# The bias of the base product as one more TensorE pass per half

## The reference, cut to what matters

```python
x = x + autocorrelation(layernorm(x), ctx, ctx)            # part a
x = x + ffn0(layernorm(x), W_base, b_base, W_router, A, B)  # part b
x = x + window_attention(layernorm(x), ctx, Wq, ..., bo)    # parts b and c
x = x + ffn1(layernorm(x), A, B, Wr)                        # part c
...
# inside ffn0, for the 128 rows of an item
lora_out = einsum('ner,eor->no', h * combine, B_stack) * SCALING
base_out = xf @ W_base.T + b_base
out = base_out + lora_out
```

## Time and profile before

| what | value |
|---|---|
| three timed executions | 2021.28, 2022.52, 2024.9 us (median 2022.52) |
| the profiled execution | 2025.97 us, of it 2024.1 us in the span |
| TensorE busy | 1855.6 us, 92% of the span |
| VectorE busy | 1519.6 us, 75% |
| ScalarE busy | 1347.2 us, 67% |
| GpSimd busy | 1088.4 us, 54% |
| mean granted TensorE clock | 0.969 |

### The profile page before, as it was taken

How to read it: one execution, slowest core, us unless ns; L and a number is a source line. 1 busy time by engine, 2 the same in 40 slices (tenths; PEclk the granted TensorE clock), 3 DMA queues, 4 the chain that set the end, 5 groups by cost and what they waited for, 6 DMA issues and landing times. The chain is left out here.

```text
span 2024.1 us, 49212 instructions
## 1 busy us (share of the span) xinstructions
PE 1855.6 (92%) x18912; PEld 1131.0 (56%) x18912; DVE 1519.6 (75%) x4529; ACT 1347.2 (67%) x1958; POOL 1088.4 (54%) x902
## 2 busy tenths in 40 slices
PE   4889999999999999999999999999999999999975
PEld 2355555665555655555565655566555565655543
DVE  6677777778777778777877777777777877877743
ACT  4267776677776677776667777667777666777652
POOL 2565555466555466555556655546655645655541
PEclk8899999999999999999999999999999999999985
DMA  5001110011111011111001111001111110111000
GB/s 217 22 33 53 52 52 31 31 52 41 52 52 36 27 50 41 52 52 52 31 31 43 50 52 52 31 31 49 45 52 52 44 39 31 41 52 42 21 6 17
DMA packets 25165, 91.56 MB, mean 45 GB/s; under 512 B 3184, under 2 KB 3312, under 8 KB 24624
## 3 DMA queue, kind: packets, MB, share of 16 engines
q1 hardware_dynamic: 25136, 91.17, 12.8%
HBM read 74.39 MB, written 16.78 MB: 45 GB/s over the span
## 5 line engine op out<-in xcount | busy, mean ns | idle before, releaser
L548 PE MATMUL pb<-w_base_h,even_words 128*128 128x512 f16 x1024 | 324.8, 379 | 0.4 <-ACT mid_t L851 0.4
L1370 POOL TENSOR_TENSOR p_hl<-sc,p_hl 128x512 f16<-128x512 f32 x128 | 178.1, 1391 | 180.3 <-ACT p_hl L730 180.3
L450 PE MATMUL pa<-ctx_a,tab 128*128 128x512 f32 x384 | 203.4, 655 | 35.6 <-ACT q_spec L730 24.3
L840 ACT ACTIVATE q_diag<-sc,par 32x1024 f32<-32x1024 f32 x192 | 216.1, 1141 | 19.9 <-DVE sc L1100 17.5
L1413 POOL TENSOR_TENSOR sc<-sc,sc_rec 128x512 f32<-128x512 f32 x128 | 134.2, 1048 | 146.8 <-DVE sc_rec L1176 146.8
L548 PE MATMUL pb<-w_base_l,even_words 128*128 128x512 f16 x512 | 193.9, 379 | 0.0
L617 PEld LDWEIGHTS pc<-sc_t,v_diag 128*128 128x128 f16 x6144 | 173.8, 97 | 32.9 <-issue 23.8
L450 PE MATMUL pa<-xn_a,tab 128*128 128x512 f32 x384 | 186.3, 609 | 1.5 <-ACT xn_a L730 1.5
L617 PE MATMUL pc<-sc_t,v_diag 128*128 128x32 f16 x6144 | 173.9, 177 | 6.5 <-ACT rows_c L730 6.5
L594 PE MATMUL pc<-k_h,q_diag 128*128 128x32 f16 x2048 | 169.1, 177 | 0.0
L595 PE MATMUL pc<-k_l,q_diag 128*128 128x32 f16 x2048 | 168.5, 177 | 0.0
(11 more groups left out here) (149 smaller groups left out, 5068.5 us busy)
## 6 DMA issues: line engine op xcount, KB each, us to landing
x_a<-in_x SPq DMA_DIRECT2D x32, 512.0 KB, 3.3
ctx_a<-in_ctx_in SPq DMA_DIRECT2D x32, 512.0 KB, 3.2
x_res<-in_x SPq DMA_DIRECT2D x32, 512.0 KB, 3.9
ctx_b<-in_ctx_in SPq DMA_DIRECT2D x32, 512.0 KB, 4.0
out<-rows_c SPq DMA_DIRECT2D x32, 512.0 KB, 2.9
v_diag<-in_base_w SPq DMA_DIRECT2D x4, 1024.0 KB, 10.1
tab<-in_spectra SPq DMA_DIRECT2D x1, 576.0 KB, 5.2
q_diag<-in_ra SPq DMA_DIRECT2D x1, 544.0 KB, 13.8
```

The costliest lines, as they stand in the source:

```text
L450: last = mm(place[:, n + h, :], lhsT, moving[:, h * HALF:(h + 1) * HALF], start=True, stop=True)
L548: mm(pb[:, h, :], rows[:, cols], weights[:, j, h * HALF:(h + 1) * HALF], start=(j == 0 and m == 0), stop=False)
L840: nc.scalar.activation(q_diag[rows, :, col:col + QB], source, ACT.Copy, scale=par[rows, a:a + 1]).then_inc(qd_out.sem, 1)
L1370: g_.tensor_tensor(part[:, :, :, LO], sc[:, g % 2, :, :], part[:, :, :, HI], ALU.subtract)\
```

## The change

The bias no longer goes through GpSimd. It is brought into the accumulation of the base product: a stationary tile of ones (64 partitions x 128) times a moving tile that holds the bias times 256 in two fp16 parts, the high part in partition 0, the rest in partition 32, and zeros in the other 62. This pass is the first of each half and starts its accumulation.

```diff
-        bias_base = sb("bias_base", [P, D])
+        bias_hl = sb("bias_hl", [P // 2, D], F16)
+        ones_h = sb("ones_h", [P // 2, P], F16)
...
-            sp.dma_start(bias_base[:, :], base_b.partition_broadcast(P)).then_inc(const_in.sem, 16)
+            sp.dma_start(x_c[0:P // 2, :], base_b.partition_broadcast(P // 2)).then_inc(const_in.sem, 16)
...
+                if part == 0:
+                    if first(b):
+                        pe.wait_ge(bias_set.sem, 2)
+                    mm(pb[:, h, :], ones_h[:, :], bias_hl[:, h * HALF:(h + 1) * HALF], start=True, stop=False)
                 for j in range(part * KT // 2, (part + 1) * KT // 2):
...
-                           start=(j == 0 and m == 0), stop=False)
+                           start=False, stop=False)
...
             def b_base(b):
                 dve.wait_ge(mm_ffn[0].sem, mm_ffn[0].after(b))
-                dve.wait_ge(bias_added.sem, bias_added.after(b))
...
+            def split_bias():
+                v.tensor_scalar(bias_hl[0:1, :], x_c[0:1, :], W_SCALE, None, ALU.mult).then_inc(bias_set.sem, 1)
+                v.tensor_scalar(bias_hl[32:33, :], x_c[32:33, :], W_SCALE, None, ALU.mult).then_inc(bias_hi.sem, 1)
+                dve.wait_ge(bias_hi.sem, 1)
+                v.scalar_tensor_tensor(out=bias_hl[32:33, :], in0=x_c[32:33, :], scalar=W_SCALE,
+                                       in1=bias_hl[32:33, :], op0=ALU.mult, op1=ALU.subtract)\
+                    .then_inc(bias_set.sem, 1)
...
+            v.memset(ones_h[:, :], 1.0).then_inc(const_set.sem, 1)
+            v.memset(bias_hl[:, :], 0.0).then_inc(const_set.sem, 1)
...
             dve.wait_ge(const_in.sem, CONSTS_IN)
+            split_bias()
             step(1, True, True, False, True)
...
-            def b_bias(b):
-                pool.wait_ge(ln_out[1].sem, ln_out[1].after(b))
-                g_.tensor_tensor(x_b[:, :], x_b[:, :], bias_base[:, :], ALU.add).then_inc(bias_added.sem, 1)
...
-                if do_b:
-                    b_bias(b)
```

More of the change, by code:

```diff
@@ L314, in build @@
         mm_ffn = [signal(f"mm_ffn{n}") for n in range(2)]
-        bias_added = signal("bias_added")
+        bias_hi = signal("bias_hi")
+        bias_set = signal("bias_set", 2)
         x2_out = signal("x2_out")
@@ L355, in build @@
         CONSTS_IN = 16 * (len(consts) + 1)
-        CONSTS_SET = 8
+        CONSTS_SET = 10
         SPLITS = 4
```

## The result

The changed kernel is slower: median 2042.17 us (2039.29 to 2048.73, four executions) against 2021.9 (2018.87 to 2024.9) on the same chip, ratio 1.0105 with a 95% interval of 1.0075 to 1.0134. The forecast was 2045.0, range 2030 to 2063.

What follows compares the result with a forecast made beforehand. A TensorE-ScalarE ring was taken as the bound. 19.5 (30 items) + 1.7 (first and last) + 1.3 (start) = 22.5 us on 2025.97 gave 2048.5; less 3.45 for the median, 2045.0 us, range 2030 to 2063.

Steps and rivals of the forecast that it cites:

- A ring of TensorE and ScalarE: The work said to set each item's time: TensorE's part 40.4 us, ScalarE's 19.2, added passes in TensorE's part.
- a second strand: From `b_mid` over ScalarE, GpSimd and VectorE to `v_im`; delayed by one added pass, half 1's.
- The cost of a pass: Each added 64-partition pass on TensorE: 0.216 us plus 0.10 at each of two partition-count changes, 0.42 us.
- rival 2: Every partition-count change empties TensorE: pass 0.74 us, whole kernel 2065.8 us; chance 0.13.
- rival 1: Added passes free of toll at 0.216 us: 2032.2 us, or 2042 with twice the caught items; chance 0.25.
- The sign that I gave for it: In the profile after, bias-pass start distances to both neighbours together 0.62 to 0.64 us, 0.43 without toll.
- 2c - 0.18: Item growth at `a_transpose`: two passes of c less TensorE's 0.18 us wait; 0.65 us, 19.5 for 30 items.
- GpSimd's addition worth nothing: Removing GpSimd's 2.36 us bias addition per item would bring neither gain nor loss, covered by VectorE's queue.
- The start, 1.3 us: `split_bias` on VectorE between steps 0 and 1: about 3 us, 1.7 covered, 1.3 remain (bounds 0 and 3).
- The first and last items, 1.7 us: No wait to give back in the first and last item: 2c each, 1.7 us.
- The clock, six items carried: Six items with a half-clock stretch, 1.65 us each, 9.9 in all, assumed unchanged, in series as short as before.
- Rival 3: Toll-free passes, and the six half-clock items vanish: 2022.3 us, no slower than before; chance 0.12.

Runs made afterwards that it cites:

- e5: Kernel before plus four repeated base passes per item behind `b_mid`; item 60.07 us, one execution 2031.93 us.
- e6: Kernel before plus four repeated base passes per item ahead of `b_mid`; item 60.48 us, one execution 2051.89 us.
- e1: Changed kernel with the ones and bias tiles over 128 partitions instead of 64, other rows zeros; 2018.57 us against 2022.02, ratio 0.9984.
- e7: Changed kernel with each bias pass issued twice in a row; item 60.48 us, one execution 2053.87 us.
- e3: Kernel before without GpSimd's addition of the bias and the wait for it; item 59.50 us, ratio 0.9996.
- e2: Changed kernel with 128-partition ones and bias tiles and half 1's pass moved behind `b_mid`; 2024.72 us against 2022.02, ratio 1.0005.
- e4: Changed kernel without its two added passes per item, `split_bias` and loads kept; item 59.49 us, ratio 1.0009.
- e9: Changed kernel run again unaltered, with six timed executions; median 2037.47 us against 2021.29, ratio 1.0075.
- e8: Kernel before with `b_mid` moved earlier on TensorE, ahead of the fourth scores group; 2015.15 us against 2022.5, ratio 0.9961.
- e10: Kernel before with GpSimd's bias addition moved behind `root(i + 1, 0)`; item 61.34 us, one execution 2067.09 us.
- e12: Kernel before with `b_mid` earlier and GpSimd's bias addition moved directly behind `root(b, 1)`; 2010.37 us against 2020.67, ratio 0.9951.

## Why the prediction was right, and where not

* **What bounds it: right.** A ring of TensorE and ScalarE, with a second strand from `b_mid` over VectorE to `v_im`. e5 and e6 show each of them deciding in turn.
* **The cost of a pass, 0.42 us with a toll of 0.10 per change: right.** Measured 0.42, with tolls of 0.08 to 0.11 per change. The one fp32 switch in the trace of before gave it; e1 and e7 show it to be the change of the number of partitions. Full drain (rival 2, toll 0.26) and no toll (rival 1) did not happen. The sign that I gave for it, distances of "0.62 to 0.64 us" together, was wrong: it took both neighbours for base passes, but the one ahead is a router pass (0.06) or an L617 pass (0.025), and the two distances are 0.47 and 0.43. With what stood there before taken off, and 0.01 at the next pass, they give 0.41 to 0.42.
* **What reaches the time, "2c - 0.18": the mis-sized term.** TensorE gives back 0.40 per item. I took the idle time in brackets, which counts from the reported end of the last pass; that end includes the latency, which a waiting successor would have overlapped. Part of the loss is also in the first transposes behind a wait, spaced wider: 0.34 of the 0.40 lies between the start of the last record ahead of the transposes and that of the first transpose (0.76 before, 0.43 changed), 0.06 in the transposes (0.93 and 0.87). So the growth is 0.44 per item instead of 0.65. With the measured 0.43 it is 12.0 us for the 28 full items, where my sum had 19.5 for 30.
* **GpSimd's addition worth nothing: wrong by 0.10 us, without effect here.** I compared match_replace beside it and saw no difference, rightly; but the addition decides where `root` runs, and `root` slows `neg_max`; that is 0.06 of the 0.10, the rest is of unknown cause. In the changed kernel the gain lies on the strand that is not the last (0.42 - 0.10 is less than 0.44), so the trade hid it. e3 and e1 show it.
* **The start, 1.3 us: not separated.** VectorE was held 2.66 us (I had about 3). What of it reached the end is covered by half-clock differences of 3 us at the start. Traces with the same half-clock time up to the first L1092 give a rough estimate: with 20.5 us of it, that stretch is 84.3 to 84.9 us with `split_bias` (e2, e4, e9) and 82.7 to 84.0 without (e5, e8, e10, e12); with 27.3 us it is 87.1 (e1) and 86.1 (before). 1.3 us fits into this, but these kernels differ in other edits too, and it is not shown.
* **The first and last items, 1.7 us: about right.** 2.0 us against e4, in the last but one 0.90, about 2c as forecast.
* **The clock, six items carried: it held on average only.** Ten and three in two executions of the same kernel, 13.0 and 5.1 us. This is larger than most terms I worked out. In e1 the sign of a difference came out against the item; half clock is the likely reason, not a shown one. The series did not behave as I argued either: I had them as short as now, two of three, and the changed kernel had one of five and five single ones in its first trace and three single ones in the second.
* **Rival 3, no slower than before,** was wrong in this kernel; but its ingredient, a toll-free pass, gives that result within 0.2% in e1 and e2. In e2 it does so by the 0.40 us given back and not, as the rival had it, by fewer caught items: its trace has eight.

The forecast of 2045.0 against 2042.17 and 2037.47 is thus partly luck: each item was forecast 0.22 us too long, about 6 us in all, and half-clock stretches that I did not forecast made up a part of it. What stays open: the first pair of medians differs by 20.3 us, the second by 16.2, while the passes account for about 14 (12.0 in the full items and 2.0 in the first and the last two distances), and the start for perhaps 1 more. The rest, about 1 to 5 us, I ascribe to half-clock stretches in executions without a trace, which is argued and not shown.

## What to carry to other kernels

A pass on the busiest engine is priced by its start-to-start distances to both neighbours; a pass that differs from them in its number of partitions pays at each border, so give it the neighbours' height, with zeros. What a wait can give back is read from start to start too, not from the idle time printed beside it, and where two strands meet each one needs its own sum. And work on GpSimd was free here only where no VectorE instruction of the kind that waits for it stood beside it: look at the duration of the small ones there, and move the whole instruction in thought, not only its end.

## What the runs showed of the hardware that I had not expected

* A pass over 64 partitions between passes over 128 costs 0.42 us instead of 0.22; two of them in a row cost 0.64 together, since the border is paid once.
* A VectorE tensor_scalar of 128x8 took 2.00 us beside a GpSimd addition of 2.37, 0.17 to 0.25 beside small GpSimd instructions (once 0.42), and 0.17 alone; match_replace and max beside the same addition lost at most 0.01.
* In the full items half clock comes in single stretches of 3.4 us, and their number changes from one execution to the next (ten and three in the changed kernel). What one costs depends on where in the item it lies: in both kernels a stretch that begins 34.4 to 34.9 us behind L1092 or L1097 costs 1.6 to 1.7 us, and one that begins 24.0 to 24.2 us behind L1097 only 0.67 to 0.76.
